# Sparsemax attention: two tiles' searches moved ahead, and the second group's candidate chain begun before the last two counts

## The chip, the core and the metric

The kernel runs on one core of one Trainium2 chip. It is one program for two decoder layers; the change touches one of its stages, the second layer's cross attention with sparsemax. The metric is the time of one execution on the device in microseconds. The core has five engines with a queue each: TensorE (PE, matrix products), VectorE (DVE), ScalarE (ACT), GpSimd (POOL) and SyncE (SP, which issues transfers). An engine works off its instructions in the order in which they are written, and waits where a semaphore has not been reached.

## The reference, cut to what matters

32 sequences, 100 queries each (S), 361 context rows each (S2), 16 heads of 16 (D = 256).

```python
def sparsemax(x):
    x = x - jnp.max(x, axis=-1, keepdims=True)
    zs = -jnp.sort(-x, axis=-1)
    ...
    support = zs > cssv / rho
    k = jnp.maximum(jnp.sum(support, axis=-1, keepdims=True), 1)
    tau = jnp.take_along_axis(cssv, k - 1, axis=-1) / k.astype(x.dtype)
    return jnp.clip(x - tau, 0.0)
...
qh = _split_heads(q @ Wq + bq)
kh = _split_heads(k @ Wk + bk)
vh = _split_heads(v @ Wv + bv)
scores = jnp.einsum('bhqd,bhkd->bhqk', qh, kh) * scale
attn = sparsemax(scores)
out = jnp.einsum('bhqk,bhkd->bhqd', attn, vh)
```

The result goes through Wo, is added to the stage's input and normalized by rows. Each row of 361 scores needs its own threshold tau, with the sum of max(x - tau, 0) equal to 1.

## The kernel before

The stage is `packed_sparse_attention`. The 16 x 100 rows of scores of one sequence lie in NT = 13 tiles of 128 rows (the last has 64) by 361. They form two groups: tiles 0 to 6 (group 0) and 7 to 12 (group 1). The threshold is found without a sort:

- `largest` (L3034) searches each tile in 8 parts of 45 or 46 scores with MAX8, 8 instructions per tile, and leaves 64 candidates per row. `half` splits a tile's search into two times 4.
- The chain of a group on VectorE: `bound` 0 and 1 (L3050, L3053) make a first threshold, `refine(.., 0, j)` and `refine(.., 1, j)` (L3063 to L3087) improve it twice. Ahead of each refine GpSimd subtracts the threshold from the candidates (`compare`, L2629). At the end stands nt0 (L3087).
- ScalarE's `cut` (L2888) subtracts nt0 from the whole tile, clips at 0 and sums. VectorE's `number` step 0 (L3096) counts what is left. `update` of step 0 or 2 (L3118, L3122, L3128) makes nu1 out of both.
- ScalarE's `excess` (L2896) and `sign` (L2904) sum and count above nu1; five tiles are counted by VectorE instead (`number` step 1: tiles 4, 5, 6, 11, 12). `update` of step 1 or 3 (L3117, L3118, L3122, L3126) makes nu2.
- GpSimd's `probability` (L2639) subtracts nu2 from each tile. TensorE turns the tiles (`turn`, L2763), ScalarE copies them out of PSUM (`copy_turned`, L2914), and TensorE multiplies by the values (`values`, L2775) and by Wo (`project_out`).

The scores come from `scores` on TensorE (L2749, L2745), in the order ORDER, through three PSUM banks: position pos needs the copy of position pos - 3. ScalarE's `copy_scores` (L2880) moves them to SBUF and counts in `z_in`, and `largest` waits for that count. The projections of a later sequence go through one bank: `turn_x`, `project_q`, `project_k` 0 and 1; `copy_x`, `copy_q`, `copy_k` 0 and 1 empty it. `project_k(.., 1)` waits for `copy_k(.., 0)`. `project_v` 0 to 2 share the bank `yo`, which `copy_v` on VectorE empties (L3023). `part_heads` on GpSimd (L2621, two instructions) spreads the queries by head.

Each engine has a `sequence(m, u)`, the body for one sequence of the batch (n = 2m + u), called by `passes`: a loop over m = 1 to 14 with u = 0 and 1, and the first and last bodies written out around it. In it `here` is work on (m, u), `behind` on the sequence before, `ahead` on the following one and `later` on the one after that. The first half of a body holds the chain of group 1 of (m, u), the second half the chain of group 0 of the following sequence. The order on each engine is written out by hand. What each wait names decides the rest: `update` step 1 and 3 wait for `total_done`, counted at the last excess of a group; `compare` for `tc_done`; `probability` of a group's first tile for nu2. GpSimd's order is: probabilities 7 to 12 of the sequence before, part_heads twice, compare of group 1 twice, add_bias, probabilities 0 to 6, compare of group 0 twice, norm. It is not changed.

## Time and profile before

| | us |
|---|---|
| three runs | 4212.95, 4183.81, 4180.03 |
| median | 4183.81 |
| the profiled execution | 4193.01 |
| its span | 4191.2 |
| VectorE busy, whole span | 2278.8 (54%) |
| ScalarE busy | 2184.1 (52%) |
| TensorE matmul busy | 3225.6 (77%) |

The stage runs from about 2180 to 3500 us, 32 bodies of some 40 us. In a row of a group "busy, mean ns | idle before <- who ended it" tells how long the engine stood just before these instructions. A row of a timeline gives the start, the duration, the engine, the line, what is written and read, and in brackets the idle time before. Names such as sa_s carry the stage's prefix; sa_nt is nt0, sa_nu is nu1 or nu2, sa_tc the threshold among the candidates, sa_sc the banks of the scores.

### The profile page before, as it was taken

To read this page: it belongs to the slowest core of one execution; us is meant where nothing else is said; L and a number is where in the kernel's file an instruction comes from. 1 tells how busy PE (TensorE), PEld (TensorE's weight loads), DVE (VectorE), ACT (ScalarE), POOL (GpSimd) and SP (SyncE) were. 2 spreads that over 40 slices of the span, in tenths; PEclk is the share of its full clock that TensorE was granted. 3 is DMA by queue.
4 is the path that set the end of the run, shared out by engine and by line. 5 is a ranking of instruction groups with operands and counts; after the bars stand their busy time and mean duration, and the time that the engine had idled before them with its cause. 6 is when DMAs were issued, how large, how long until landed. Compare 5 with 4: busy or idle time off the path is not lost. (4 is left out here: it accounts for less than half of the span.)

```text
span 4191.2 us, 84333 instructions
## 1 busy us (share of the span) xinstructions
PE 3225.6 (77%) x21166; PEld 1996.2 (48%) x21166; DVE 2278.8 (54%) x10359; ACT 2184.1 (52%) x6653; POOL 1448.4 (35%) x2228
## 2 busy tenths in 40 slices
PE   7999987888988824887767777877777775687772
PEld 5566665566666512444434444444444444344441
DVE  1222222566666684667648888888888882211112
ACT  3433333566566602666637877877777783221110
POOL 1111111355455545455523444444343441110005
PEclk9999998899999966768767887888888785899996
DMA  1000000111111011000010000000000003206773
GB/s 62 19 12 12 14 15 29 36 38 38 34 37 39 20 38 49 19 19 22 18 38 18 16 18 20 16 18 16 18 19 16 18 8 113 90 33 203 223 228 110
DMA packets 111870, 189.32 MB, mean 45 GB/s; under 512 B 11150, under 2 KB 95886, under 8 KB 105550
## 3 DMA queue, kind: packets, MB, share of 16 engines
q1 hardware_dynamic: 102094, 166.32, 12.9%
q10 hardware_dynamic: 7200, 14.68, 0.9%
q0 software_dynamic: 2400, 6.56, 0.5%
q14 instruction: 137, 1.12, 0.1%
q8 instruction: 39, 0.64, 0.1%
HBM read 149.90 MB, written 37.62 MB: 45 GB/s over the span
## 5 line engine op out<-in xcount | busy, mean ns | idle before, releaser
L3034 DVE MAX8 sa_cand<-sa_s 128x8 f32<-128x45 f32 (+3 forms) x3328 | 404.1, 191 | 34.7 <-ACT sa_s L2880 31.8
L852 ACT ACTIVATE ca_p<-ca_sm,ca_nb 100x361 f32<-100x361 f32 x512 | 301.9, 591 | 210.8 <-DVE ca_nb L936 209.8
L2763 PE MATMUL sa_tr<-sa_ident,sa_s 128*128 128x128 f32 (+3 forms) x1248 | 277.3, 339 | 167.9 <-POOL sa_s L2639 90.8
L672 POOL TENSOR_SCALAR ca_p<-ca_p,ca_rec 100x361 f32<-100x361 f32 x512 | 286.7, 579 | 345.2 <-DVE ca_rec L950 344.9
L2639 POOL TENSOR_SCALAR sa_s<-sa_s,sa_unit,sa_nu 128x361 f32<-128x361 f32 (+1 forms) x416 | 261.3, 644 | 306.3 <-DVE sa_nu L3126 306.3
L2763 PEld LDWEIGHTS sa_tr<-sa_ident,sa_s 128*128 128x128 f32 (+3 forms) x1248 | 185.5, 178 | 268.4 <-issue 257.5
L2888 ACT ACTIVATE sa_s<-sa_s,sa_nt 128x361 f32<-128x361 f32 (+1 forms) x416 | 244.3, 592 | 97.2 <-DVE sa_nt L3087 97.2
L936 DVE CUSTOM_DVE_ANT_0 ca_sm<-ca_sc,ca_mb 100x361 f32<-100x361 f32 x512 | 252.3, 526 | 69.4 <-PE ca_sc L759 56.4
L2896 ACT ACTIVATE sa_spare_a<-sa_s,sa_nu 128x361 bf16<-128x361 f32 (+1 forms) x416 | 247.2, 595 | 64.8 <-DVE sa_nu L3128 64.8
L2629 POOL TENSOR_TENSOR sa_over<-sa_cand,sa_tc 128x280 f32<-128x280 f32 (+3 forms) x128 | 99.3, 776 | 451.6 <-DVE sa_tc L3053 272.8
L2749 PE MATMUL sa_sc<-sa_kT,sa_qm 32*128 32x361 f32 (+3 forms) x768 | 227.2, 522 | 22.1 <-ACT sa_s L2880 21.5
L2914 ACT ACTIVATE sa_pT<-sa_tr 128x512 f32<-128x512 f32 (+5 forms) x384 | 182.7, 498 | 100.2 <-PE sa_tr L2763 97.2
L770 PEld LDWEIGHTS ca_tr<-ca_ident,ca_p 100*128 100x128 f32 (+1 forms) x1536 | 172.0, 154 | 102.3 <-issue 73.5
L770 PE MATMUL ca_tr<-ca_ident,ca_p 100*128 100x100 f32 (+1 forms) x1536 | 209.0, 260 | 3.2 <-POOL ca_p L672 2.5
L3096 DVE TENSOR_SCALAR_CACHE_REDUCE sa_spare_d<-sa_s 128x361 bf16<-128x361 f32 (+1 forms) x416 | 202.9, 517 | 0.1
L2728 PE MATMUL sa_yo<-sa_wv,sa_cTs 128*128 128x256 f32 (+1 forms) x384 | 157.9, 552 | 52.6 <-DVE sa_vm L3023 52.6
L465 DVE TENSOR_TENSOR ta_vpre<-ta_proj,ta_bvs 100x512 f32<-100x512 f32 x64 | 44.3, 692 | 276.0 <-PE ta_proj L337 275.9
L2880 ACT ACTIVATE sa_s<-sa_sc 128x361 f32<-128x361 f32 (+1 forms) x416 | 178.4, 464 | 20.1 <-PE sa_sc L2749 15.1
L1626 ACT ACTIVATE na_p<-na_sm,na_nb 100x100 f32<-100x100 f32 x512 | 186.8, 376 | 1.9 <-DVE na_nb L1691 0.7
L285 POOL TENSOR_SCALAR_AFFINE_SELECT ta_pT<-ta_pT 100x400 f32<-100x400 f32 x128 | 67.9, 542 | 318.4 <-ACT ta_pT L428 314.1
L1457 POOL TENSOR_TENSOR na_rs<-na_rs,na_half 100x32 f32<-100x32 f32 x32 | 174.5, 5453 | 2.7
L2749 PEld LDWEIGHTS sa_sc<-sa_kT,sa_qm 32*128 32x128 f32 (+3 forms) x768 | 82.9, 183 | 157.1 <-ACT sa_s L2880 94.2
(323 smaller groups left out, 7755.8 us busy)
## 6 DMA issues: line engine op xcount, KB each, us to landing
ea_we<-m_experts SPq DMA_DIRECT2D x40, 1024.0 KB, 6.6
ea_wd<-m_experts SPq DMA_DIRECT2D x40, 512.0 KB
ca_cTs<-cT SPq DMA_DIRECT2D x32, 361.0 KB
sa_cTs<-cT SPq DMA_DIRECT2D x32, 361.0 KB
rows_in<-me_zeros ACTq DMA_DIRECT2D x1, 7168.0 KB
ea_xe<-rows_in SPq DMA_DIRECT2D x40, 128.0 KB
rows_out<-ea_ye ACTq DMA_DIRECT2D x40, 128.0 KB
ca_ms<-mask SPq DMA_DIRECT2D x32, 141.0 KB
```

Source lines behind the costliest of these rows:

```text
L672: ins = pool.tensor_scalar(p[:, r, j, :], p[:, r, j, :], rec[:, r, j:j + 1], 1.0, ALU.mult, ALU.mult)
L770: mm = pe.transpose(tr[f % 2][0:kn, j * S:(j + 1) * S], p[:, r, j, k0:k0 + kn], ident[0:S, 0:S])
L852: act.activation(p[:, r, j, :], sm[:, r % 2, j, :], ACT.Exp, bias=nb[:, r % 2, j:j + 1], scale=-1.0, accum_out=den[:, r, j:j + 1]).then_in ...
L936: dve.tensor_tensor_reduce(sm[:, r % 2, j, :], sc[j][0:S, 0:S2], mb[:, u, :], -1 / 4, 3e38, ALU.add, ALU.min, nb[:, r % 2, j:j + 1]).then_ ...
L1626: act.activation(p[:, r, j, :], sm[:, r, j, :], ACT.Exp, bias=nb[:, r, j:j + 1], scale=-1.0, accum_out=den[:, r, j:j + 1]).then_inc(exp_do ...
L2639: pool.tensor_scalar(s[0:rows, u, i, :], s[0:rows, u, i, :], unit[0:rows, :], nu2[0:rows, i:i + 1], ALU.mult, ALU.add).then_inc(p_done.sem, 1)
L2749: mm = pe.matmul(bank[0:rows, 0:S2], qm[hr, u, P * i:P * i + rows], kT[hr, u, i // 7, :], start=True, stop=True)
L2763: mm = pe.transpose(tr[f % 2][0:kn, c0:c0 + rows], s[0:rows, u, i, k0:k0 + kn], ident[0:rows, 0:rows])
L2888: act.activation(s[0:rows, u, i, :], s[0:rows, u, i, :], ACT.Relu, bias=nt0[0:rows, i:i + 1], accum_out=total[0:rows, i:i + 1]).then_inc(r ...
L2896: ins = act.activation(spare_a[0:rows, i, :], s[0:rows, u, i, :], ACT.Relu, bias=nu1[0:rows, i:i + 1], accum_out=total[0:rows, i:i + 1])
L3034: ins = dve.max(cand[0:rows, i, q, :], s[0:rows, u, i, PART[q]:PART[q + 1]])
L3096: ins = dve.tensor_scalar(spare_d[0:rows, i, :], s[0:rows, u, i, :], u1[0:rows, i:i + 1] if step else 0.0, 0.0, ALU.is_gt, ALU.add, accum_ ...
```

## The change

On VectorE, the searches of positions 7 and 8 move from the head of a body to the end of the body before, between the steps of the chain of group 0. Group 1's searches now end sooner: its `bound` stands ahead of the counts of tiles 5 and 6, `copy_v(.., 0)` and `update` step 0; refine and update take turns. The searches of positions 0 and 1 of the following sequence move into group 1's chain. In the second half group 0's `bound` stands ahead of the count of tile 12 and of `update` step 2. On ScalarE, the copies of positions 0 to 2 stand among the excesses 1 to 3, and those of positions 7 to 9 among the excesses 9 to 11, ahead of both copy_k. On TensorE, scores 0 to 2 stand ahead of project_v(.., 1), scores 7 to 9 ahead of values(.., 0). The same instructions are issued per pass of the loop.

The diff, with its indentation cut by 12:

```diff
--- before.py
+++ after.py
@@ -2800,6 +2800,9 @@
             turn(*before, 2, t)
         for t in range(NK):
             turn(*before, 3, t)
+    if ahead:
+        for i in range(3):
+            scores(*following, i)
     if here:
         project_v(m, u, 1)
     if behind:
@@ -2807,10 +2810,6 @@
         values(*before, 3)
     if here:
         project_v(m, u, 2)
-    if ahead:
-        for i in range(3):
-            scores(*following, i)
-
     if ahead:
         for i in range(3, 7):
             scores(*following, i)
@@ -2826,6 +2825,10 @@
     if here:
         for t in range(NK):
             turn(m, u, 1, t)
+    if ahead:
+        for i in range(7, 10):
+            scores(*following, i)
+    if here:
         values(m, u, 0)
     if later:
         project_k(*second, 0)
@@ -2833,9 +2836,6 @@
         values(m, u, 1)
     if later:
         project_k(*second, 1)
-    if ahead:
-        for i in range(7, 10):
-            scores(*following, i)
 
 for u in range(2):
     turn_x(0, u)
@@ -2925,8 +2925,6 @@
     before = prev(m, u)
 
     if here:
-        for i in range(7, 10):
-            copy_scores(m, u, i)
         for i in range(3):
             cut(m, u, i)
             copy_scores(m, u, 10 + i)
@@ -2942,20 +2940,19 @@
     if behind:
         copy_turned(*before, 3, 1)
         copy_turned(*before, 3, 2)
-    if here:
-        for i in range(1, 4):
+    for i in range(1, 4):
+        if ahead:
+            copy_scores(*following, i - 1)
+        if here:
             excess(m, u, i)
             sign(m, u, i)
+    if here:
         excess(m, u, 4)
     if behind:
         copy_out(*before)
     if here:
         excess(m, u, 5)
         excess(m, u, 6)
-
-    if ahead:
-        for i in range(3):
-            copy_scores(*following, i)
     for i in range(4):
         if here:
             cut(m, u, 7 + i)
@@ -2979,25 +2976,26 @@
         copy_turned(m, u, 1, 1)
         sign(m, u, 8)
         copy_turned(m, u, 1, 2)
-        excess(m, u, 9)
-        sign(m, u, 9)
+    for i in range(7, 10):
+        if ahead:
+            copy_scores(*following, i)
+        if here:
+            excess(m, u, i + 2)
+            if i < 9:
+                sign(m, u, i + 2)
     if later:
         copy_k(*second, 0)
     if here:
-        excess(m, u, 10)
-        sign(m, u, 10)
-        excess(m, u, 11)
+        excess(m, u, 12)
     if later:
         copy_k(*second, 1)
-    if here:
-        excess(m, u, 12)
 
 for u in range(2):
     copy_x(0, u)
     copy_q(0, u)
     copy_k(0, u, 0)
     copy_k(0, u, 1)
-for i in range(7):
+for i in range(10):
     copy_scores(0, 0, i)
 passes(act, sequence)
 
@@ -3152,108 +3150,119 @@
     if behind:
         update(*before, 3, late, 0)
     if here:
-        largest(m, u, 7, 0)
+        largest(m, u, 9, 0)
     if behind:
         update(*before, 3, late, 1)
     if here:
-        largest(m, u, 7, 1)
+        largest(m, u, 9, 1)
     if behind:
         update(*before, 3, late, 2)
     if here:
-        largest(m, u, 8)
         number(m, u, 0, 0)
-        largest(m, u, 9)
+        largest(m, u, 10)
         number(m, u, 1, 0)
+        largest(m, u, 11)
         number(m, u, 2, 0)
-        largest(m, u, 10, 0)
+        largest(m, u, 12, 0)
         number(m, u, 3, 0)
         number(m, u, 4, 0)
-        largest(m, u, 10, 1)
+        largest(m, u, 12, 1)
+        bound(m, u, 1, second, 0)
         number(m, u, 5, 0)
+        bound(m, u, 1, second, 1)
         number(m, u, 6, 0)
+        copy_v(m, u, 0)
         update(m, u, 0, chain, 0)
-        largest(m, u, 11, 0)
+        refine(m, u, 1, 0, second, 0)
         update(m, u, 0, chain, 1)
-        largest(m, u, 11, 1)
+        refine(m, u, 1, 0, second, 1)
         update(m, u, 0, chain, 2)
-        largest(m, u, 12)
-        copy_v(m, u, 0)
-        bound(m, u, 1, second, 0)
+        refine(m, u, 1, 0, second, 2)
         number(m, u, 4, 1)
-        bound(m, u, 1, second, 1)
-        number(m, u, 5, 1)
-        refine(m, u, 1, 0, second, 0)
-        refine(m, u, 1, 0, second, 1)
-        refine(m, u, 1, 0, second, 2)
         copy_v(m, u, 1)
         refine(m, u, 1, 0, second, 3)
+        number(m, u, 5, 1)
         refine(m, u, 1, 0, second, 4)
         number(m, u, 6, 1)
+    if ahead:
+        largest(*following, 0)
+    if here:
         refine(m, u, 1, 1, second, 0)
         refine(m, u, 1, 1, second, 1)
+    if ahead:
+        largest(*following, 1, 0)
+    if here:
         refine(m, u, 1, 1, second, 2)
         copy_v(m, u, 2)
-        for j in range(3, 7):
-            refine(m, u, 1, 1, second, j)
-
+        refine(m, u, 1, 1, second, 3)
+        refine(m, u, 1, 1, second, 4)
+    if ahead:
+        largest(*following, 1, 1)
     if here:
+        refine(m, u, 1, 1, second, 5)
+        refine(m, u, 1, 1, second, 6)
         update(m, u, 1, chain, 0)
     if ahead:
-        largest(*following, 0, 0)
+        largest(*following, 2, 0)
     if here:
         update(m, u, 1, chain, 1)
     if ahead:
-        largest(*following, 0, 1)
+        largest(*following, 2, 1)
     if here:
         update(m, u, 1, chain, 2)
-    if ahead:
-        largest(*following, 1)
-    if here:
         number(m, u, 7, 0)
-    if ahead:
-        largest(*following, 2)
-    if here:
-        number(m, u, 8, 0)
-        number(m, u, 9, 0)
     if ahead:
         largest(*following, 3)
     if here:
-        number(m, u, 10, 0)
-        number(m, u, 11, 0)
+        number(m, u, 8, 0)
     if ahead:
-        largest(*following, 4, 0)
+        largest(*following, 4)
     if here:
-        number(m, u, 12, 0)
-        update(m, u, 2, chain, 0)
-    if ahead:
-        largest(*following, 4, 1)
-    if here:
-        update(m, u, 2, chain, 1)
+        number(m, u, 9, 0)
     if ahead:
         largest(*following, 5, 0)
     if here:
-        update(m, u, 2, chain, 2)
+        number(m, u, 10, 0)
+        number(m, u, 11, 0)
     if ahead:
         largest(*following, 5, 1)
         largest(*following, 6)
         bound(*following, 0, first, 0)
     if here:
+        number(m, u, 12, 0)
+    if ahead:
+        bound(*following, 0, first, 1)
+    if here:
+        update(m, u, 2, chain, 0)
+    if behind:
+        output(*before)
+    if here:
+        update(m, u, 2, chain, 1)
+    if ahead:
+        refine(*following, 0, 0, first, 0)
+    if here:
+        update(m, u, 2, chain, 2)
+    if ahead:
+        refine(*following, 0, 0, first, 1)
+    if here:
         number(m, u, 11, 1)
     if ahead:
-        bound(*following, 0, first, 1)
-    if behind:
-        output(*before)
-    if ahead:
-        refine(*following, 0, 0, first, 0)
-        refine(*following, 0, 0, first, 1)
         refine(*following, 0, 0, first, 2)
-        refine(*following, 0, 0, first, 3)
-        refine(*following, 0, 0, first, 4)
     if here:
         number(m, u, 12, 1)
     if ahead:
-        for j in range(7):
-            refine(*following, 0, 1, first, j)
+        refine(*following, 0, 0, first, 3)
+        refine(*following, 0, 0, first, 4)
+        largest(*following, 7)
+        refine(*following, 0, 1, first, 0)
+        refine(*following, 0, 1, first, 1)
+        largest(*following, 8, 0)
+        refine(*following, 0, 1, first, 2)
+        refine(*following, 0, 1, first, 3)
+        refine(*following, 0, 1, first, 4)
+        largest(*following, 8, 1)
+        refine(*following, 0, 1, first, 5)
+        refine(*following, 0, 1, first, 6)
 
 for i in range(7):
     largest(0, 0, i)
@@ -3264,6 +3273,8 @@
     refine(0, 0, 0, 0, first, j)
 for j in range(7):
     refine(0, 0, 0, 1, first, j)
+largest(0, 0, 7)
+largest(0, 0, 8)
 passes(dve, sequence)
 dve.wait_ge(*worst_done.at(B, 0))
 dve.tensor_reduce(top[:, :], worst[:, :], AX.X, ALU.max).then_inc(top_step, 1)
```

In the new program VectorE's functions stand 2 lines higher up (L3034 is L3032); those of ScalarE keep their numbers.

**VectorE, second half of a body**, from refine(.., 1, 0) of group 0 to the next body's first instructions. Before:

```order
L3096 TENSOR_SCALAR sa_spare_d,sa_count<-sa_s,sa_u 64x361
L3063 TENSOR_SCALAR sa_over<-sa_over 128x7x64
L3064 TENSOR_SCALAR sa_over<-sa_over 128x7x64
L3067 TENSOR_REDUCE sa_both<-sa_over 128x14
L3070 RECIPROCAL sa_few<-sa_both 128x7
L3073 SCALAR_TENSOR_TENSOR sa_shift<-sa_both,sa_few 128x7
L3076 TENSOR_TENSOR sa_tc<-sa_tc,sa_shift 128x7
L3083 TENSOR_SCALAR sa_low<-sa_tc 128x7
```

Now:

```order
L3074 TENSOR_TENSOR sa_tc<-sa_tc,sa_shift 128x7
L3032 MAX sa_cand<-sa_s 128x8 x8
L3061 TENSOR_SCALAR sa_over<-sa_over 128x7x64
L3062 TENSOR_SCALAR sa_over<-sa_over 128x7x64
L3065 TENSOR_REDUCE sa_both<-sa_over 128x14
L3032 MAX sa_cand<-sa_s 128x8 x4
L3068 RECIPROCAL sa_few<-sa_both 128x7
L3071 SCALAR_TENSOR_TENSOR sa_shift<-sa_both,sa_few 128x7
L3074 TENSOR_TENSOR sa_tc<-sa_tc,sa_shift 128x7
L3032 MAX sa_cand<-sa_s 128x8 x4
L3081 TENSOR_SCALAR sa_low<-sa_tc 128x7
```

The eight MAX8 ahead of L3061 are the search of position 7, the four and four behind it that of position 8.

**ScalarE, end of a body**, behind the excesses and signs of tiles 7 and 8 (L2896, L2904), up to the loop's branch. Before:

```order
L2914 ACTIVATE sa_pT<-sa_tr 105x384
L2896 ACTIVATE sa_spare_a,sa_total<-sa_s,sa_nu 128x361
L2904 ACTIVATE sa_spare_s,sa_signs<-sa_s,sa_nu 128x361
L2871 ACTIVATE sa_kT<-sa_proj,sa_bks 128x361
L2896 ACTIVATE sa_spare_a,sa_total<-sa_s,sa_nu 128x361
L2904 ACTIVATE sa_spare_s,sa_signs<-sa_s,sa_nu 128x361
L2896 ACTIVATE sa_spare_a,sa_total<-sa_s,sa_nu 128x361
L2871 ACTIVATE sa_kT<-sa_proj,sa_bks 128x361
L2896 ACTIVATE sa_spare_a,sa_total<-sa_s,sa_nu 64x361
L2597 UNCONDITIONAL_BRANCH
```

Now:

```order
L2914 ACTIVATE sa_pT<-sa_tr 105x384
L2880 ACTIVATE sa_s<-sa_sc 128x361
L2896 ACTIVATE sa_spare_a,sa_total<-sa_s,sa_nu 128x361
L2904 ACTIVATE sa_spare_s,sa_signs<-sa_s,sa_nu 128x361
L2880 ACTIVATE sa_s<-sa_sc 128x361
L2896 ACTIVATE sa_spare_a,sa_total<-sa_s,sa_nu 128x361
L2904 ACTIVATE sa_spare_s,sa_signs<-sa_s,sa_nu 128x361
L2880 ACTIVATE sa_s<-sa_sc 128x361
L2896 ACTIVATE sa_spare_a,sa_total<-sa_s,sa_nu 128x361
L2871 ACTIVATE sa_kT<-sa_proj,sa_bks 128x361
L2896 ACTIVATE sa_spare_a,sa_total<-sa_s,sa_nu 64x361
L2871 ACTIVATE sa_kT<-sa_proj,sa_bks 128x361
```

The three score copies (L2880) stand behind the last copy_turned, and one excess instead of an excess, a sign and an excess lies between the two copy_k (L2871).

**TensorE, first half of a body**, behind the transposes of the sequence before (L2763). Before:

```order
L2763 MATMUL sa_tr<-sa_ident,sa_s 105x64
L2728 MATMUL sa_yo<-sa_wv,sa_cTs 128x256 x2
L2775 MATMUL sa_ov<-sa_pT,sa_vm 32x100 x24
L2728 MATMUL sa_yo<-sa_wv,sa_cTs 105x256 x2
L2749 MATMUL sa_sc<-sa_kT,sa_qm 128x361 x6
```

Now:

```order
L2763 MATMUL sa_tr<-sa_ident,sa_s 105x64
L2749 MATMUL sa_sc<-sa_kT,sa_qm 128x361 x3
L2728 MATMUL sa_yo<-sa_wv,sa_cTs 128x256 x2
L2775 MATMUL sa_ov<-sa_pT,sa_vm 32x100 x24
L2728 MATMUL sa_yo<-sa_wv,sa_cTs 105x256 x2
L2749 MATMUL sa_sc<-sa_kT,sa_qm 128x361 x3
```

Three of the six scores (L2749) now stand ahead of project_v(.., 1), the first L2728.

## Rows read from the trace of the kernel before

**Rows 1.** Window table of two bodies: span, busy PE, PEld, DVE, ACT, POOL, clock, DMA
```profile
2800.10:2842.00 41.90, 31.55 (x209) 18.32 (x207) 33.81 (x197) 35.02 (x109) 16.86 (x25) 0.88 0.07 22
2842.00:2881.12 39.12, 30.24 (x195) 17.50 (x195) 33.92 (x196) 28.81 (x90) 16.86 (x25) 0.74 0.04 13
```

**Rows 2.** The same view of three short stretches
```profile
2809.00:2812.00 3.00, 2.11 (x6) 1.43 (x5) 2.69 (x18) 2.75 (x10) 0.55 (x1) 0.50 0.00 0
2816.00:2820.00 4.00, 2.56 (x12) 0.89 (x6) 3.12 (x12) 2.17 (x6) 0.17 (x1) 1.00 0.40 118
2842.00:2848.00 6.00, 2.80 (x9) 1.71 (x10) 5.80 (x43) 2.90 (x10) 4.12 (x7) 0.50 0.00 1
```

**Rows 3.** Groups of VectorE, 2250 to 3390 us: count, busy us, mean ns, idle before
```profile
L3063 DVE TENSOR_SCALAR sa_over<-sa_over 128x384 f32<-128x384 f32 x29 | 25.1, 867 | 15.6 <-POOL sa_over L2629 15.6
...
L3122 DVE SCALAR_TENSOR_TENSOR sa_u<-sa_total,sa_rec 128x7 f32<-128x7 f32 x28 | 16.3, 581 | 0.0
...
L3063 DVE TENSOR_SCALAR sa_over<-sa_over 128x448 f32<-128x448 f32 x28 | 11.9, 425 | 18.2 <-POOL sa_over L2629 18.2
...
L3070 DVE RECIPROCAL sa_few<-sa_both 128x7 f32<-128x7 f32 x56 | 11.3, 201 | 8.2
...
L3117 DVE TENSOR_SCALAR sa_count<-sa_signs 128x4 f32<-128x4 f32 x57 | 9.7, 170 | 43.4 <-issue 42.9
...
L3063 DVE TENSOR_SCALAR sa_over<-sa_over 128x240 f32<-128x240 f32 x28 | 8.0, 285 | 11.1 <-POOL sa_over L2629 11.1
```

**Rows 4.** VectorE's timeline in the first of these bodies: start us, us, instruction
```profile
2809.07 0.15 DVE L3128 TENSOR_SCALAR sa_nu<-sa_u 128x7 f32<-128x7 f32 x1
...
2813.66 0.42 DVE L3023 TENSOR_TENSOR sa_vm<-sa_yo,sa_bvs 128x256 f32<-128x256 f32 x1
...
2819.49 0.17 DVE L3117 TENSOR_SCALAR sa_count<-sa_signs 128x4 f32<-128x4 f32 x1
...
2827.89 0.15 DVE L3128 TENSOR_SCALAR sa_nu<-sa_u 128x6 f32<-128x6 f32 x1
```

**Rows 5.** GpSimd's timeline in the same body, with the idle time before in brackets
```profile
2801.95 3.77 POOL L2639 TENSOR_SCALAR sa_s<-sa_s,sa_unit,sa_nu 128x361 f32<-128x361 f32 x6 [2.82 <-DVE sa_nu L3126]
...
2805.69 3.00 POOL L2621 TENSOR_TENSOR sa_qm<-sa_qs,sa_hm 128x800 f32<-128x800 f32 x2
...
2811.45 0.63 POOL L2629 TENSOR_TENSOR sa_over<-sa_cand,sa_tc 128x240 f32<-128x240 f32 x1 [2.77 <-DVE sa_tc L3053]
```

**Rows 6.** Timeline of all engines at 2191 us, the stage's start
```profile
2191.30 1.52 POOL L2621 TENSOR_TENSOR sa_qm<-sa_qs,sa_hm 128x800 f32<-128x800 f32 x1
2191.38 1.73 DVE L3063 TENSOR_SCALAR sa_over<-sa_over 128x448 f32<-128x448 f32 x1 [1.15 <-POOL sa_over L2629]
```

**Rows 7.** ScalarE's timeline in the body of rows 4
```profile
2809.25 0.60 ACT L2896 ACTIVATE sa_spare_a<-sa_s,sa_nu 128x361 bf16<-128x361 f32 x1 [1.18 <-DVE sa_nu L3128]
...
2816.55 1.20 ACT L2880 ACTIVATE sa_s<-sa_sc 128x361 f32<-128x361 f32 x3
...
2828.07 0.59 ACT L2896 ACTIVATE sa_spare_a<-sa_s,sa_nu 128x361 bf16<-128x361 f32 x1 [1.18 <-DVE sa_nu L3128]
...
2831.97 0.60 ACT L2896 ACTIVATE sa_spare_a<-sa_s,sa_nu 128x361 bf16<-128x361 f32 x1
...
2836.33 1.18 ACT L2880 ACTIVATE sa_s<-sa_sc 128x361 f32<-128x361 f32 x3
```

**Rows 8.** TensorE's timeline in the body of rows 4
```profile
2807.97 1.58 PE L2763 MATMUL sa_tr<-sa_ident,sa_s 128*128 128x128 f32 x4 [0.27 <-ACT sa_pT L2914]
...
2810.44 2.08 PE L2728 MATMUL sa_yo<-sa_wv,sa_cTs 128*128 128x256 f32 x4 [0.89 <-DVE sa_vm L3023]
...
2815.65 0.88 PE L2749 MATMUL sa_sc<-sa_kT,sa_qm 32*128 32x361 f32 x6
...
2833.74 1.48 PE L2716 MATMUL sa_proj<-sa_cTs,sa_wk 128*128 128x361 f32 x4 [0.61 <-ACT sa_kT L2871]
```

## The prediction

> **What bounds the kernel now.** I read the window table first, to see what a pass of the loop costs: 81.02 us for two bodies (41.90 and 39.12 us) in which VectorE is busy 33.8 and 33.9 us; over the pair that is 67.7 us, against 63.8 of ScalarE, 61.8 of TensorE and 33.7 of GpSimd [rows 1]. Then the groups of VectorE over 1140 us of the stage [rows 3]: its listed idle time is 43.4 us at L3117, put down to "issue" (14 times, once per pass of the loop, 3.1 us each: no engine releases it), and 11.1 + 15.6 + 18.2 = 44.9 us at L3063, where it waits for GpSimd's compare (some 1.6 us per body). It never stands waiting for ScalarE or TensorE. The rest, some 3.6 us per body, are waits of 0.15 us between small operations of its own chain (8.2 us over 56 at L3070, [rows 3]). Then the timelines. VectorE's halves of a body run from L3117 to L3117: 2800.10, 2819.49, 2842.00, that is 19.4 us and 19.4 us + 3.1 us of the loop's turn [rows 1, 4]. ScalarE stands 1.2 us ahead of its first excess [rows 7] and GpSimd 2.8 us ahead of its probabilities [rows 5], both for VectorE. So VectorE's order is the bound, and what the edit can gain is its small gaps. The question is who is late next.
>
> I count t from the L3117 that opens a body, T from the one that opens its second half.
>
> **The VectorE work alone.** The edit adds and removes nothing within a pass: 104 MAX8, 13 + 5 counts, three copy_v. It only puts searches and counts between chain steps. By my count it covers six or seven of the small waits in a half (0.15 us each) and some 0.5 us of compare waits, 1.5 us in all: 17.9 us instead of 19.4 if nobody else were late. That would be 3.0 us per body. Four waits take its place.
>
> **First half, ScalarE's end.** nu1, which starts the seven excesses, is written at t = 9.1 now (L3128, 2809.07 + 0.15) [rows 4]. In the new order update(0, 1) and (0, 2) stand behind refine(.., 0), which waits for GpSimd's compare of the second group. GpSimd takes nu2 at t = 1.85, six probabilities (3.77 us) and two part_heads (3.00 us), so it is free at t = 8.6 and not before [rows 5]; the compare (0.63 us) can end at 9.25. Behind it come L3063, L3064, the update's two steps with the reduce between them (0.65 us): some 1.35 us, so nu1 at 10.6. There is one unknown. bound(.., 1) (L3053) would issue at t = 7.2, in the second part_heads (7.1 to 8.6). No row has L3053 beside one, but two show VectorE held up there: L3063 took 1.73 us at the stage's start beside a part_heads of 1.52 us [rows 6], against 0.43 in the loop, and L3122 takes 0.58 us in each body where it falls beside the second part_heads [rows 3]. So its price is 0 to 1.4 us for L3053, and as the compare was waiting anyway, 0 to 0.4 us for nu1. I take the block: nu1 at 11.0.
>
> The Trainium skill says of this in "SBUF — State Buffer", Who interferes with whom, that a tensor_scalar of VectorE can take both ports, and that whichever of it and a GpSimd operation comes second fully blocks. The rows above agree for the wide L3063; no row shows it for seven elements. By the rule the block is certain and this end of the first half 19.4 us; without it nu1 is at 10.6 and the end at 19.1.
>
> From nu1 ScalarE needs 7.3 us now to the end of the seventh excess (2809.25 to 2816.55) [rows 7]. The edit puts three score copies between them, 0.36 us apart (1.20 us for three), so 8.4 us: total_done at t = 19.4 (19.1 without the block). update(1) can't start before it. Now it starts at 19.39, with ScalarE ready at 16.6. **The saving of the first half is gone: 0 to 0.3 us.**
>
> **First half, TensorE's end.** scores 0 to 2 now stand ahead of project_v(1). The transposes end at 9.45 (2807.97 + 1.58) [rows 8]. The three scores took 0.88 us, at a granted clock of at most 1.00; at this place the stretch 2809 to 2812 shows 0.50 [rows 2, 8], so 0.9 to 1.8 us. project_v(1) took 2.08 us at that clock. So its copy_v(1) comes at t = 12.4 to 13.3 instead of 11.3 to 11.7 where VectorE gets to it; I take 12.8. What stands behind copy_v(1) on VectorE up to update(1) is 5.83 us now (2813.66 to 2819.49) [rows 4]; with count 5 (0.50), the searches of tiles 0 and 1 (16 MAX8, 1.75 us) added, and 1.5 us of waits covered, 6.6 us. That gives t = 19.4 too. Both ends agree: **first half 19.5 us**.
>
> **Second half.** VectorE reaches largest(7) at about T = 12.5: bound, output, refine 0 to 4 with both counts. It needs copy_scores(7). ScalarE does that behind excess 7, sign 7, copy_turned, copy_q, excess 8 and so on: 3.90 us behind its start (2828.07 to 2831.97) [rows 7]. That start waits for nu1 of the second group, now at T = 8.55 (2827.89 + 0.15 less 2819.49) [rows 4], but moved behind bound, output (1.2 us) and L3063: T = 10.3. So copy 7 ends at 10.3 + 3.9 + 0.46 = T 14.7, **and VectorE waits 2.2 us for it**. Of this 0.5 us come back, as the compare's wait is hidden behind it. 17.9 + 2.2 − 0.5 = **19.6 us against 19.4**. ScalarE's own end is close: from nu1 to the end of excess 12 it needs 8.3 us now (to 2836.33), + 1.08 for the copies − 0.45 for the copy_k that moved behind it + 0.2 for the accumulator: T = 19.4.
>
> **Across the bodies.** copy_k(.., 0) ends at T = 10.3 + 8.33 = 18.7. Only then may TensorE begin project_k(.., 1) (1.48 us, [rows 8]), which has just excess 12 to hide it now, where three operations of 1.7 us did. copy_k(.., 1) follows at 20.4 to 20.8, and cut 0 after it, 1.2 us behind VectorE's next start. The count of tile 0 waits 0.5 us, and everything that follows the cuts (copy_turned of the body before, the transposes) is late by 1.2 us: transposes end at 10.5, copy_v(1) at 13.8, **first half 20.4 us**. After the loop's turn, whose 3.1 us I leave as they are (same branch, same length of loop), this delay is hidden.
>
> **Sum** for a pass: 19.5 + 19.6 (u = 0), 20.4 + 19.6 + 3.1 (u = 1) = 82.2 to 82.3 against 81.0 (39.12, and 41.90 with the turn). 14 passes: +17 us, and 2 to 3 us for the four bodies outside the loop, in two of which the late copy_k counts too. The profiled execution's own time is 4193.0 us (span 4191.2), so 4213; the median of the three runs shown is 9 us lower, so I give 4184 + 20 = **4204 us**.
>
> **The rivals.**
> *A, the searches really cover the gaps.* copy 7 is there in time, and neither scores nor nu1 delay anyone: 3.0 us in each of 32 bodies, 4184 − 96 = 4088 us. Against it stands ScalarE's order, where copy 7 has 3.9 us of work ahead of it: it holds only if those excesses start 2 us earlier than nu1 lets them. 3%.
> *B, ScalarE alone limits* (first half 19.1 without the block, second 19.4, VectorE catching up in the loop's turn at 17.9 + 3.1): 78.6 us per pass, −2.5 us, over 16 passes −40 us, 4144 us. It needs TensorE's scores at the full clock and VectorE past copy 7 sooner. 7%.
> *C, both small delays absent* (no block, project_k(1) hidden): 19.3 + 19.6 + 19.3 + 22.7 = 80.9, −3 us in all, 4181 us. 22%.
> *D, slower.* One mechanism: TensorE stands idle for about 3 us ahead of project_k(.., 1), and its clock falls from 1.00 to 0.50, as it has in the stretch 2842 to 2848, where TensorE is busy for 2.80 of 6 us [rows 2]. Against it: in 2816 to 2820 it is busy for 2.56 of 4 us and stays at 1.00. Then project_k takes 2.9 us, copy_k and all cuts of u = 1 come 1.4 us later still: +2.7 us per pass, +43 us in all, 4227 us; with the scores and project_v at their late end (13.3) in both bodies, 0.5 us more each, 4243. It decides once project_k(1) takes over 2.4 us. 18%.
> *My forecast*, 50%: 4184 to 4215.
>
> **Numbers.** About 1% (42 us) is what a measurement of this kernel tells from no change. Faster by more than that: A and half of B, with some for what I have not seen: 0.09. Slower: most of D: 0.15. Range 4144 to 4238: B's end and D's are inside, A and the worst of D out. The forecast's own range is 4184 to 4215.
>
> **What would show it.** In the profile after: a wait at the searches of VectorE (MAX8) for ScalarE's score copy, of some 2 us per body, which is absent now; L3053 (L3051 then) lasting 1 to 1.5 us in the second group; ScalarE's wait ahead of its first excess grown from 1.2 to about 2.7 us; VectorE's waits at the compare mostly gone; a new wait of copy_v for TensorE. If VectorE's halves are 18 us, my ScalarE order is wrong and A holds; if the body of u = 1 takes over 44 us, D holds.

## The result and the profile after

| | before | after |
|---|---|---|
| median of the runs of one session, us | 4186.8 (4 runs, 4180.03 to 4212.95) | 4229.9 (4 runs, 4219.64 to 4239.82) |
| ratio to before | 1 | 1.0092, 95% interval 1.0057 to 1.0127 |
| the profiled execution, its span | 4193.01, 4191.2 | 4228.55, 4226.7 |
| from the first to the last start of a half in the stage | 1264.1 | 1313.7 |

The changed kernel is about 1% slower. All of it lies in the stage (+49.5 us). What lies ahead of the stage was 9.7 us shorter in this execution, though no instruction there changed; the first start of a half lies anywhere from 2200 to 2232 us in the profiled executions of all the kernels here, and 8 us apart in the two of one and the same kernel (e7, e10), so from here on passes of the loop are compared and not spans.

VectorE's halves of a body, from one `update(..)` count (L3117 before, L3115 after: the file is two lines shorter there) to the next, mean over the 14 passes:

| us | before | predicted | after |
|---|---|---|---|
| u = 0, first half | 19.66 | 19.5 | 19.36 |
| u = 0, second | 19.45 | 19.6 | 21.31 |
| u = 1, first | 19.40 | 20.4 | 20.06 |
| u = 1, second, with the loop's turn | 22.48 | 22.7 | 23.72 |
| a pass | 81.00 | 82.2 to 82.3 | 84.45 |

The window table of two bodies of after, u = 1 and then u = 0 (columns as in [rows 1]: span, busy PE, PEld, DVE, ACT, POOL, granted clock, DMA share, GB/s), with two stretches of 4 us in those bodies:

```profile
2814.09:2857.83 43.74, 34.00 (x212) 18.23 (x212) 32.67 (x195) 34.05 (x106) 17.11 (x25) 0.85 0.06 16
2857.83:2899.05 41.22, 34.30 (x196) 19.46 (x197) 33.67 (x195) 30.48 (x93) 16.70 (x25) 0.67 0.06 17
2892.00:2896.00 4.00, 4.00 (x30) 2.11 (x29) 2.81 (x12) 3.75 (x13) 1.57 (x4) 0.50 0.10 27
2845.00:2849.00 4.00, 2.55 (x23) 1.21 (x25) 1.98 (x8) 4.00 (x14) 1.43 (x3) 1.00 0.00 0
```

Against [rows 1] VectorE is busy for 66.3 us per pair instead of 67.7, and the pair takes 84.96 us instead of 81.02. So it does not do more; it waits more. Where, the groups of VectorE over 2250 to 3390 us tell (count, busy us, mean ns, idle before and who ended it), the same window as in [rows 3]:

```profile
L3032 DVE MAX8 sa_cand<-sa_s 128x8 f32<-128x45 f32 (+1 forms) x2810 | 345.6, 191 | 67.3 <-ACT sa_s L2880 65.9
L3094 DVE TENSOR_SCALAR_CACHE_REDUCE sa_spare_d<-sa_s 128x361 bf16<-128x361 f32 (+1 forms) x352 | 177.9, 517 | 12.2 <-ACT sa_s L2888 11.2
L3061 DVE TENSOR_SCALAR sa_over<-sa_over 128x280 f32<-128x280 f32 (+1 forms) x108 | 45.4, 420 | 0.9 <-POOL sa_over L2629 0.3
L3021 DVE TENSOR_TENSOR sa_vm<-sa_yo,sa_bvs 128x256 f32<-128x256 f32 (+1 forms) x81 | 33.0, 407 | 38.6 <-PE sa_yo L2728 38.5
L3115 DVE TENSOR_SCALAR sa_count<-sa_signs 128x4 f32<-128x4 f32 x54 | 9.2, 171 | 57.1 <-issue 42.5 <-ACT sa_spare_a L2896 14.1
```

The 44.9 us at the compare (L3063 in [rows 3], L3061 here) are gone. In their place stand 65.9 us of searches that wait for a score copy, 38.5 us of `copy_v` that waits for TensorE, 14.1 us of the update and 11.2 us of counts that wait for ScalarE: none of the four is there before, when VectorE never waited for ScalarE or TensorE.

### The profile page after: what moved, and what is told of

It reads as the page before. It is cut to its first block and busy times, and to the rows that moved or that the text cites. A ratio compares the mean times of both kernels' runs of the same rounds, so it can differ in the third digit from the quotient of the medians.

```text
span 4226.7 us, 84361 instructions
## 1 busy us (share of the span) xinstructions
PE 3259.2 (77%) x21166; PEld 2006.7 (47%) x21166; DVE 2257.9 (53%) x10359; ACT 2182.5 (52%) x6653; POOL 1454.1 (34%) x2228
## 5 line engine op out<-in xcount | busy, mean ns | idle before, releaser
L3032 DVE MAX8 sa_cand<-sa_s 128x8 f32<-128x45 f32 (+3 forms) x3328 | 408.1, 192 | 108.8 <-ACT sa_s L2880 107.3
L2763 PE MATMUL sa_tr<-sa_ident,sa_s 128*128 128x128 f32 (+3 forms) x1248 | 244.7, 315 | 170.7 <-ACT sa_pT L2914 137.5
L2896 ACT ACTIVATE sa_spare_a<-sa_s,sa_nu 128x361 bf16<-128x361 f32 (+1 forms) x416 | 248.0, 598 | 136.4 <-DVE sa_nu L3126 136.4
L2763 PEld LDWEIGHTS sa_tr<-sa_ident,sa_s 128*128 128x128 f32 (+3 forms) x1248 | 173.2, 168 | 244.3 <-issue 225.7
L2749 PE MATMUL sa_sc<-sa_kT,sa_qm 32*128 32x361 f32 (+3 forms) x768 | 268.1, 657 | 15.9 <-ACT sa_s L2880 15.9
L3094 DVE TENSOR_SCALAR_CACHE_REDUCE sa_spare_d<-sa_s 128x361 bf16<-128x361 f32 (+1 forms) x416 | 210.1, 517 | 14.3 <-ACT sa_s L2888 13.2
L2880 ACT ACTIVATE sa_s<-sa_sc 128x361 f32<-128x361 f32 (+1 forms) x416 | 192.4, 464 | 14.6 <-PE sa_sc L2745 7.7
L1535 PE MATMUL na_tr<-na_ident,na_p 100*100 100x100 f32 x512 | 85.4, 301 | 91.0 <-DVE na_p L1705 87.5
L1691 DVE CUSTOM_DVE_ANT_0 na_sm<-na_sc,na_cm 100x100 f32<-100x100 f32 x512 | 127.2, 261 | 49.3 <-PE na_sc L1524 30.8
```

The costliest lines, as they stand in the source:

```text
L2749: mm = pe.matmul(bank[0:rows, 0:S2], qm[hr, u, P * i:P * i + rows], kT[hr, u, i // 7, :], start=True, stop=True)
L2763: mm = pe.transpose(tr[f % 2][0:kn, c0:c0 + rows], s[0:rows, u, i, k0:k0 + kn], ident[0:rows, 0:rows])
L2880: act.activation(s[0:rows, u, i, :], sc[pos % SC][0:rows, 0:S2], ACT.Copy).then_inc(z_in.sem, 1)
L2896: ins = act.activation(spare_a[0:rows, i, :], s[0:rows, u, i, :], ACT.Relu, bias=nu1[0:rows, i:i + 1], accum_out=total[0:rows, i:i + 1])
L3032: ins = dve.max(cand[0:rows, i, q, :], s[0:rows, u, i, PART[q]:PART[q + 1]])
L3094: ins = dve.tensor_scalar(spare_d[0:rows, i, :], s[0:rows, u, i, :], u1[0:rows, i:i + 1] if step else 0.0, 0.0, ALU.is_gt, ALU.add, accum_ ...
```

## How a late nu1 comes back as a late search

The timeline of VectorE in the body of u = 0 (start, duration, and in brackets the idle time before); it answers to [rows 4]:

```profile
2857.83 0.17 DVE L3115 TENSOR_SCALAR sa_count<-sa_signs 128x4 f32<-128x4 f32 x1 [3.35 <-issue]
...
2868.50 0.16 DVE L3126 TENSOR_SCALAR sa_nu<-sa_u 128x7 f32<-128x7 f32 x1
...
2870.66 0.42 DVE L3021 TENSOR_TENSOR sa_vm<-sa_yo,sa_bvs 128x256 f32<-128x256 f32 x1 [1.26 <-PE sa_yo L2728]
...
2877.16 0.17 DVE L3115 TENSOR_SCALAR sa_count<-sa_signs 128x4 f32<-128x4 f32 x1
...
2887.98 0.16 DVE L3126 TENSOR_SCALAR sa_nu<-sa_u 128x6 f32<-128x6 f32 x1
...
2893.05 0.95 DVE L3032 MAX8 sa_cand<-sa_s 128x8 f32<-128x45 f32 x8 [2.64 <-ACT sa_s L2880]
...
2899.05 0.17 DVE L3115 TENSOR_SCALAR sa_count<-sa_signs 128x4 f32<-128x4 f32 x1 [0.99 <-ACT sa_spare_a L2896]
```

The same stretch on ScalarE ([rows 7] before):

```profile
2868.69 0.60 ACT L2896 ACTIVATE sa_spare_a<-sa_s,sa_nu 128x361 bf16<-128x361 f32 x1 [2.86 <-DVE sa_nu L3126]
...
2888.17 0.60 ACT L2896 ACTIVATE sa_spare_a<-sa_s,sa_nu 128x361 bf16<-128x361 f32 x1 [2.11 <-DVE sa_nu L3126]
...
2892.43 0.47 ACT L2880 ACTIVATE sa_s<-sa_sc 128x361 f32<-128x361 f32 x1 [0.25 <-PE sa_sc L2749]
...
2897.80 0.56 ACT L2871 ACTIVATE sa_kT<-sa_proj,sa_bks 128x361 f32<-128x361 f32 x1 [1.30 <-PE sa_proj L2716]
2898.26 0.59 ACT L2896 ACTIVATE sa_spare_a<-sa_s,sa_nu 64x361 bf16<-64x361 f32 x1
```

And on TensorE ([rows 8] before):

```profile
2889.95 0.94 PE L2763 MATMUL sa_tr<-sa_ident,sa_s 128*105 128x128 f32 x3 [3.01 <-ACT sa_pT L2914]
2890.82 3.08 PE L2749 MATMUL sa_sc<-sa_kT,sa_qm 64*128 64x361 f32 x6
2893.83 1.23 PE L2775 MATMUL sa_ov<-sa_pT,sa_vm 128*32 128x100 f32 x24
2894.99 2.78 PE L2716 MATMUL sa_proj<-sa_cTs,sa_wk 128*128 128x361 f32 x4
```

In the kernel before the same transposes came after 2.08 us of idle time:

```profile
2829.86 0.55 PE L2763 MATMUL sa_tr<-sa_ident,sa_s 128*105 128x128 f32 x3 [2.08 <-ACT sa_pT L2914]
```

Read together: nu1 of the second half is written at T = 10.8 instead of 8.4 (2887.98 less 2877.16). ScalarE has stood idle for 2.11 us by then, with `copy_turned(1, 0)` queued behind excess 7. TensorE waits 3.01 us for that copy. Its last transposes start at T = 12.8 in all 14 bodies of u = 0, and in the kernel before at T = 10.35 to 10.6 in eleven of them and at 12.0 in three: mostly 2.2 to 2.4 us later now, as nu1 is. In this body TensorE then comes back at the lower clock: the last transposes, the scores 7 to 9 and `project_k(.., 0)` take 0.94, 3.08 and 2.78 us where the body ahead of it (u = 1) shows 0.55, 1.68 and 1.48 at 1.00:

```profile
2846.67 0.55 PE L2763 MATMUL sa_tr<-sa_ident,sa_s 128*105 128x128 f32 x3 [1.45 <-ACT sa_pT L2914]
2847.14 1.68 PE L2749 MATMUL sa_sc<-sa_kT,sa_qm 64*128 64x361 f32 x6
2848.75 0.73 PE L2775 MATMUL sa_ov<-sa_pT,sa_vm 128*32 128x100 f32 x24
2849.41 1.48 PE L2716 MATMUL sa_proj<-sa_cTs,sa_wk 128*128 128x361 f32 x4
```

So copy 7 and both copy_k come late, search 7 waits 2.64 us, and excess 12, which stands behind `copy_k(.., 0)`, ends late too: the update waits for it.

The body of u = 1 shown here is not the rule for its kind. Over the 14 passes in the trace of after, the first project_k of a second half takes 2.3 to 2.8 us in all 14 bodies of u = 0 and in 12 of u = 1. Before, it did so in 5 of the 28, and then nobody waited for it. In one of the five the half took 19.45 us like every other of u = 0:

```profile
2466.70 0.94 PE L2763 MATMUL sa_tr<-sa_ident,sa_s 128*105 128x128 f32 x3 [2.15 <-ACT sa_pT L2914]
...
2468.72 2.78 PE L2716 MATMUL sa_proj<-sa_cTs,sa_wk 128*128 128x361 f32 x4
```

In after the scores 7 to 9, which search 7 is waiting for, stand in this stretch. The half of u = 0 goes with them: it takes 20.34 and 20.43 us in the two bodies where these scores took 1.94 and 2.02 us, and 21.4 to 21.9 us in the nine where they took 3.1 us.

The first half has a second cause, on GpSimd ([rows 5] before): `bound(.., 1)` now falls beside part_heads.

```profile
2865.11 1.36 DVE L3051 TENSOR_SCALAR sa_tc<-sa_level 128x6 f32<-128x6 f32 x1
```
```profile
2863.44 3.00 POOL L2621 TENSOR_TENSOR sa_qm<-sa_qs,sa_hm 128x800 f32<-128x800 f32 x2
2866.64 0.63 POOL L2629 TENSOR_TENSOR sa_over<-sa_cand,sa_tc 128x240 f32<-128x240 f32 x1 [0.21 <-DVE sa_tc L3051]
```

VectorE's L3051 ends at 2866.47, GpSimd's pair at 2866.44. Six elements took 1.36 us here and 0.92 us on average over 27 bodies; before, 0.157 us over 28. In e2 and e12, where searches 7 and 8 stand in the first half, this bound starts at t = 9.0, behind part_heads (over at t = 8.6), and takes 0.17 us.

## The experiments

The change has three parts: **S**, the searches of positions 0 and 1 in group 1's chain, with scores 0 to 2 and their copies ahead; **T**, searches 7 and 8 in group 0's chain, with scores and copies 7 to 9 and the place of copy_k; and **C**, the chain begun ahead of the last two counts (both `bound`) with update and refine step about. "nu1" is the mean time over the 14 passes from the start of a half to the start of the operation that writes nu1. **S'** is S in another form: scores 0 to 2 stand behind project_v(1) and ahead of `values(.., 2)` instead of ahead of project_v(1), and their copies one excess later.

| kernel | parts | median us (runs) | ratio to before, 95% | pass us | nu1, first and second half |
|---|---|---|---|---|---|
| before | none | 4186 to 4191 | 1 | 81.00 | 8.98, 8.39 |
| e7_before01 | S' | 4148.12 (4) | 0.9890, 0.9847 to 0.9934 | 78.35 | 8.98, 7.60 |
| e10_again | S' | 4140.60 (6) | 0.9885, 0.9855 to 0.9916 | 78.42 | 8.98, 7.60 |
| e11_search4 | S', T | 4135.54 (4) | 0.9876, 0.9849 to 0.9903 | 78.71 | 9.12, 7.61 |
| e12_chain | C | 4203.06 (10) | 1.0034, 1.0012 to 1.0056 | 82.36 | 11.23, 12.64 |
| e2_tail | S, C | 4186.27 (10) | 1.0005, 0.9983 to 1.0027 | 81.27 | 11.23, 10.70 |
| e3_head | T, C | 4244.60 (4) | 1.0136, 1.0084 to 1.0189 | 84.70 | 10.74, 12.64 |
| after | S, T, C | 4229.90 (4) | 1.0092, 1.0057 to 1.0127 | 84.45 | 10.75, 10.70 |

e1 to e4 undo or move one thing in the changed kernel; the others follow from what these leave open.

**e1_copyk**: is it the late copy_k? The order of copy_k and excesses as before, in the changed kernel.

```diff
-    for i in range(7, 10): copy_scores(i); excess(i + 2); sign
-    copy_k(0); excess(12); copy_k(1)
+    copy_scores(7); excess(9); sign(9); copy_k(0)
+    copy_scores(8); excess(10); sign(10); copy_scores(9); excess(11)
+    copy_k(1); excess(12)
```

> The changed kernel with ScalarE's two copy_k where they stood before: copy_k 0 ahead of excess 10, copy_k 1 ahead of excess 12; the score copies 7 to 9 stay among the excesses. Theory 1 (TensorE is late with project_k, because scores 7 to 9 now stand ahead of it and its clock is low in the body u = 0): copy_k 0 now waits ahead of excesses 10 to 12 instead of behind them, the second half of u = 0 grows from 21.3 to 22 to 23.5 us, the pass from 84.4 to 85 to 86, total +10 to +25 us. Rival (as in the prediction: only copy_k 1 behind excess 12 is late): cuts of u = 1 start in time, first half of u = 1 from 20.1 to 19.4, second half of u = 0 from 21.3 to 20.3, pass 82.7, total -28 us.

Measured: 4301.99 us (ratio 1.0274, 1.0225 to 1.0324), a pass of 88.91 us, second halves of 23.94 and 26.22. ScalarE's queue now waits for project_k at an earlier place, and copies 8 and 9, which VectorE wants, stand behind it:

```profile
L3039 DVE MAX8 sa_cand<-sa_s 128x8 f32<-128x45 f32 (+1 forms) x2672 | 328.7, 191 | 127.6 <-ACT sa_s L2880 126.1 <-issue 0.2
```

126.1 us against 65.9 of after, and a loss of 4.5 us per pass where theory 1 expected 0.6 to 1.6. In one place the rival was right: the first half of u = 1 falls from 20.06 to 19.41 us, so the late copy_k costs 0.65 us there. What a late copy_k costs in the second halves e1 doesn't show, because copies 8 and 9 now stand behind it; with the scores moved ahead on TensorE, copy_k is rightly put behind the copies.

**e2_tail**: part T undone.

```diff
-    scores(7..9); values(0); project_k(0); values(1); project_k(1)
+    values(0); project_k(0); values(1); project_k(1); scores(7..9)
     (copies 7 to 9, copy_k and searches 7 and 8 likewise as before)
```

> The changed kernel with its second-half part undone: searches 7 and 8 back at the head of a body, score copies 7 to 9 behind excess 12, scores 7 to 9 behind project_k 1, copy_k as before; the group-1 chain ahead of the counts, scores, copies and searches 0 to 2 and the chain of the second half stay. Theory 1 (the loss lies in the second half: VectorE waits for copy 7, TensorE late): second halves 21.3 and 20.6 + 3.1 go to about 19.0 and 17.4 + 3.1, first halves 19.7 to 20; pass 79, total 4150 to 4165 us, faster than the kernel before. Rival (the loss is in the first half: scores ahead of project_v, VectorE held up at bound): second halves hardly change the total, first halves rise by the 1.75 us of the two searches to 21.1 and 21.8; pass 82 to 83, total above 4200.

Measured: 4186.27 us, the time of before; a pass of 81.27. The sign was right and the hoped-for gain of the first part is absent: u = 0's second half takes 20.46 us instead of 19.45. This 1 us goes with the clock: in the three bodies where project_k(.., 0) took 1.48 us the half took 19.5 us, in the eleven where it took 2.2 to 2.8 us 20.3 to 21.8 us. VectorE's groups show what it waits for at the update:

```profile
L3117 DVE TENSOR_SCALAR sa_count<-sa_signs 128x4 f32<-128x4 f32 x56 | 9.5, 170 | 95.6 <-ACT sa_spare_a L2896 66.2 <-issue 29.3
```

66.2 us for the seventh and the last excess: ScalarE's chain from nu1 is now the bound of a half.

**e3_head**: part S undone.

```diff
-    refine(1,1,0..1) with largest(0), largest(1) between up to refine(1,1,6)
+    refine(1, 1, 3..6); update(1, ..) with largest(0), largest(1) between
     (scores 0 to 2 and their copies as before)
```

> The changed kernel with its first-half part undone: scores 0 to 2 back behind project_v 2, score copies 0 to 2 behind excess 6, searches 0 and 1 behind update 1; the rest as changed. Theory 1: copy_v 1 waits for TensorE no more and the first half falls to about 18.5 us, but the second half takes the two searches (1.75 us) and nu1 comes that much later, so copy 7 too: second half 21.5 to 23; pass 83 to 85, total within 20 us of the changed kernel. Rival (TensorE's scores ahead of project_v are the loss): pass back to 81 to 82, total 4190.

Measured: a pass of 84.70 us, 4244.60. The first halves fall to 18.21 and 18.41 us, and the second ones rise to 22.70 and 25.38: the 1.75 us of searches go back there. S is not what costs: beside T and C it still gains 0.25 us per pass.

**e4_early**: the updates of both groups ahead of the refine steps (and ahead of `output`), so that nu1 comes earlier; all else as in the changed kernel.

```diff
+    update(0, 0); copy_v(0); update(0, 1); update(0, 2)
     refine(1, 0, 0..1)
     ...
+    update(2, 0); update(2, 1); update(2, 2)
     output(before); refine(0, 0, 0..)
```

> The changed kernel with the updates whole and early: update(0, 0 to 2) ahead of refine(.., 0) in the first half, update(2, 0 to 2) ahead of output in the second. Theory 1 (nu1 starts ScalarE's excesses and with them everything that ends a half): nu1 1 us earlier in the first half, which TensorE's copy_v 1 then holds at 19.3; 1.2 to 1.7 us earlier in the second, of which ScalarE can use 0.6 to 1.0: pass 82.4 to 83, total -25 us against the changed kernel. Rival (VectorE's own amount of work bounds it): the uncovered small waits cost 0.5 us per body, total +15 us.

Measured: 4192.65 us (10 runs; ratio 1.0013, 0.9991 to 1.0036), a pass of 81.75, more than expected. nu1 comes at 10.12 and 9.44 instead of 10.75 and 10.70. The waits of after shrink at both ends, here VectorE's searches and ScalarE's first excess (116.6 us at L2896 in the changed kernel, 56.5 before):

```profile
L3032 DVE MAX8 sa_cand<-sa_s 128x8 f32<-128x45 f32 (+1 forms) x2912 | 357.8, 191 | 11.9 <-ACT sa_s L2880 7.9
```
```profile
L2896 ACT ACTIVATE sa_spare_a<-sa_s,sa_nu 128x361 bf16<-128x361 f32 (+1 forms) x362 | 217.4, 602 | 56.1 <-DVE sa_nu L3126 56.1
```

nu1 is 1.25 us earlier in the second half, and 1.75 us come back in u = 0's (21.31 to 19.56): the rest is TensorE, whose scores 7 to 9 take 1.68 us again in nine of the 14 bodies of u = 0 (a half of 19.3 us), and 2.9 to 3.0 us in the other five (20.1 us).

**e5_warm**: is the clock alone the cause? The transposes of turn(1, 1) issued seven times over (same result), which fills TensorE's idle time.

```diff
+    for _ in range(6 if (q, t) == (1, 1) else 0):
+        the transposes of this turn once more
```

> The changed kernel with added work on TensorE alone: the transposes of turn(.., 1, 1) are issued seven times instead of once (18 more), into the same bank, in the stretch where TensorE stands idle for about 3 us. ScalarE fetches that bank some 4 us later. Theory 2 (in the body u = 0 the granted clock falls to 0.50 in this idle stretch, and scores 7 to 9, the values and project_k 0 take twice as long, which delays copy_k 0, excess 12 and the cuts): clock 1.00 in the second half of u = 0, project_k 0 in 1.5 us instead of 2.8, second half of u = 0 from 21.3 to 20.2 us, pass 83.2, total -18 us. Rival (only the order on ScalarE counts, not the clock): same or slower by the added 2.5 us where TensorE is awaited, total 0 to +20 us.

Measured: a pass of 83.29 us (-1.16), u = 0's second half 20.71; the total, 4227.07 against 4229.90, can't be told from after. The clock over the window of the groups is back at before's 0.82 (0.79 in after):

```profile
2250.00:3390.00 1140.00, 930.26 (x6029) 550.43 (x6033) 912.96 (x5339) 874.64 (x2709) 469.32 (x684) 0.82 0.06 17
```

That is a third of the 3.45 us that a pass lost, and the clock's whole part is larger, because the added products hold the clock only in some bodies. Scores 7 to 9 of u = 0 take 1.68 us in eight of the 14, and their half takes 20.35 to 20.37 us; in the other six they take 2.6 to 3.0 us, and the half 21.0 to 21.4 us. So of the 1.86 us that this half lost (19.45 to 21.31) some 0.9 us are there at the full clock too, and the other 0.95 us are the clock's. nu1 hasn't moved (10.69 in the second half), and the last transposes start at T = 12.8 in all 14 as in after. The clock amplifies the delay and doesn't start it.

**e6_combo**: e4 with bound earlier, scores 0 to 2 behind project_v(1), and copies 0 to 2 one excess later (the form S').

```diff
-    scores(0..2); project_v(1)
+    project_v(1); scores(0..2)
-    number(3); number(4); largest(12, 1); bound(1, 0); number(5); bound(1, 1)
+    largest(12, 1); bound(1, 0); number(3); bound(1, 1); number(4); number(5)
```

> The changed kernel with what the theory asks for: the updates whole and early in both halves (as in e4), bound(.., 1) ahead of counts 3 and 4 so that it falls ahead of the second part_heads, TensorE's scores 0 to 2 behind project_v 1 instead of ahead of it, and score copies 0 to 2 one excess later. Theory (nu1 starts each half's end, TensorE's scores hold copy_v 1): nu1 at t = 9.0, copy_v 1 at t = 11.7, first halves 18.2 to 18.6 us instead of 19.4 and 20.1; second halves as in e4 (19.6 and 22.75) or better; pass 78.5 to 79.5, total 4145 to 4165 us, 0.5 to 1% faster than the kernel before. Rival (something else holds the halves, as the loop of ScalarE's own work): first halves stay at 19.3 and more, total 4190.

Measured: a miss, 4216.49 us and a pass of 82.80; first halves 20.30 and 20.18 instead of 18.4. nu1 of the first half comes at 10.83, later than in e4 (10.12). The second halves are those of e4 (19.58 and 22.74), and copy_v waits no more for TensorE (0.6 us over the window, 25.7 in e4, 38.5 in after). L3053 of six elements takes 1.74 us on average. Three edits are added to e4 here; e8 has one of them alone.

**e8_bound**: the changed kernel with that earlier bound alone.

> The changed kernel with one edit: search 12 whole and bound(.., 1) ahead of counts 3 and 4, so that L3051 issues at about t = 6.3, between no two operations of part_heads. Theory: L3051 of group 1 takes 0.16 us instead of 0.92, nu1 of the first half 0.3 us earlier, but copy_v 1 waits for TensorE as before, so the halves stay at 19.4 and 20.1: total within 8 us of the changed kernel. Rival (VectorE held up beside part_heads costs the first half): 0.4 us per body, -12 us or more.

Measured: 4241.27 us (1.0076 to 1.0154), a pass of 85.17, u = 0's first half 20.06 instead of 19.36, nu1 at 11.46. Both theories missed: L3051 took 1.76 us on average, not 0.16. The start is earlier and the end isn't:

```profile
2875.34 2.26 DVE L3051 TENSOR_SCALAR sa_tc<-sa_level 128x6 f32<-128x6 f32 x1
```
```profile
2874.57 3.00 POOL L2621 TENSOR_TENSOR sa_qm<-sa_qs,sa_hm 128x800 f32<-128x800 f32 x2
```

It is held for 2.26 us, to 2877.60, when both part_heads are over (2877.57), across the boundary between the two. Counted from the start of the half (2868.97) this is t = 8.6, as in after. VectorE stands for all that time with counts queued behind it. This is where e6's first halves went, at least in part.

**e7_before01**: the kernel before with part S' alone.

```diff
+    scores(0..2)         (TensorE, behind project_v(1), ahead of values(2))
+    copy_scores(0..2) among excess(2..4)             (ScalarE)
     refine(1, 1, 0..1) -> largest(0) ahead, largest(1) between and behind
     update(1, ..) -> largest(2); later ones one or two places earlier
```

> The kernel before with one part of the idea: only the searches 0 and 1 move into group 1's chain, with scores 0 to 2 behind project_v 1 and their copies among excesses 2 to 4; searches 7 to 9, their copies and scores, and all else as before. Theory: nothing waits for copy 7, nu1 of the second half comes 1.7 us earlier; first halves 19.8 (the 1.75 us of searches less the waits that they cover), second halves 18.5 to 19 and 20.2 with the loop's turn, pass 78.5 to 79.5, total 4150 to 4165. Rival (filling the chain's waits brings nothing, since ScalarE's and TensorE's work from nu1 on bounds the second half at 19.4): pass 81 to 82, total 4190 to 4200.

Measured: 4148.12 us, a pass of 78.35, 1.1% faster than before. The compare's wait:

```profile
L3064 DVE TENSOR_SCALAR sa_over<-sa_over 128x384 f32<-128x384 f32 (+1 forms) x117 | 48.8, 417 | 30.3 <-POOL sa_over L2629 30.3
```

30.3 us against the 44.9 of [rows 3], some 0.5 us per body, and no new wait. The gain shows in the second half: with two tiles' searches (1.75 us) gone from it, it gets to nu1 at 7.60 us instead of 8.39 (0.8 us earlier, not the 1.7 expected) and ends in u = 0 after 17.95 us instead of 19.45, and the first half, which took the searches in, grows by 0.33 us only. TensorE kept its clock: the first project_k of a second half takes 1.48 us in all 28.

**e9_scores**: e7 without VectorE's part, to see whether the earlier scores alone bring the gain. As in e7, the scores stand behind project_v(1), not ahead of it as the text below has it.

> The kernel before with the PE and ScalarE half of e7 alone: scores 0 to 2 ahead of project_v(1), their copies among excesses 2 to 4; VectorE's order stays that of before, so no search stands in group 1's chain. Theory (the gain of e7 is VectorE's: searches between steps of the second group's chain, which stands waiting for GpSimd's compare): without them the compare waits at L3063 stay as before (some 1.6 us per body), a pass stays at 80.5 to 81.5 us, the total at 4180 to 4200. Rival (the gain was ScalarE's and TensorE's, from scores and copies that come earlier and free the later ones): a pass of 78 to 79.5 us and a total near 4150, as e7 with 78.35 and 4148.

Measured: 4195.01 us (10 runs; ratio 1.0005, 0.9983 to 1.0027), a pass of 80.91, and the compare's wait as before:

```profile
L3064 DVE TENSOR_SCALAR sa_over<-sa_over 128x240 f32<-128x240 f32 (+1 forms) x114 | 54.5, 478 | 45.2 <-POOL sa_over L2629 45.2
```

The gain needs VectorE's order; the earlier scores and copies alone bring nothing. The rival fell.

**e10_again**: e7 once more, against chance.

> The kernel of e7 once more (the kernel before with only the searches of tiles 0 and 1 in the second group's chain, and the scores and copies that they need). Theory: its gain is a property of the order and not of one session: a ratio to before of 0.985 to 0.993, a pass of 78 to 78.8 us, second halves near 18 us in u = 0. Rival (the seven runs' difference was partly chance): a ratio of 0.995 to 1.0 and a pass over 80 us.

Measured: 4140.60 us, ratio 0.9885, a pass of 78.42, second halves of 17.94.

**e11_search4**: e7 with part T as well (S' and T); the updates and both bounds stay where they stood before.

> The kernel of e7 with the change's second-half part added: searches 7 and 8 between the steps of group 0's chain, scores 7 to 9 ahead of values 0, copies 7 to 9 among the excesses 9 to 11 and ahead of copy_k. The updates and both bounds stand where they stood before. Theory (the parts' costs add up; the second-half part costs 84.45 - 81.27 = 3.2 us per pass wherever it stands, because copy 7 comes too late and copy_k later): a pass of 81.3 to 81.8 us, total 4180 to 4195. Rival (it costs only where the late update holds nu1 of the second group back; with the update ahead of bound and output, copy 7 is there 2 us earlier, and search 7 covers gaps): a pass of 77.3 to 78.6 us, total 4120 to 4155, and no wait at MAX8.

Measured: 4135.54 us, a pass of 78.71, not 81.5. The parts don't add up: T costs 0.4 us per pass beside S' (e11 less e7), and 3.2 us beside S and C (after less e2). nu1 is at 7.61 in the second half, search 7 hardly waits and the compare's wait is a quarter of [rows 3]'s:

```profile
L3035 DVE MAX8 sa_cand<-sa_s 128x8 f32<-128x45 f32 (+1 forms) x3016 | 377.1, 192 | 12.6 <-ACT sa_s L2881 10.3
...
L3064 DVE TENSOR_SCALAR sa_over<-sa_over 128x448 f32<-128x448 f32 (+1 forms) x116 | 45.3, 391 | 11.4 <-POOL sa_over L2629 11.4
```

The rival's place was right and its size was not: it promised some more gain over e7, and e11 and e7 can't be told apart by the total. Both are 1.1 to 1.2% faster than before, and 2% faster than the changed kernel.

**e12_chain**: part C alone, both moves of searches undone.

> The change with both moves of searches undone: what is left is the chain's part alone, bound of either group ahead of the last counts, and refine and update step about, with the searches of positions 7 to 12 that much earlier in the body; TensorE and ScalarE as before. Theory (the parts add up; this one costs 81.27 - 78.35 = 2.9 us per pass through nu1, which is late): a pass of 83.5 to 84.2 us, ScalarE ahead of its first excess some 1.3 us per half later than before, total 4220 to 4235. Rival (it costs only together with the searches of tiles 0 and 1, which delay VectorE further): a pass of 80.5 to 81.5 us, total 4180 to 4195.

Measured: 4203.06 us (ratio 1.0012 to 1.0056), a pass of 82.36: between the two theories. VectorE comes to the update earlier and waits there for ScalarE, which waited for nu1:

```profile
L3115 DVE TENSOR_SCALAR sa_count<-sa_signs 128x4 f32<-128x4 f32 x55 | 9.4, 170 | 80.8 <-ACT sa_spare_a L2893 51.6 <-issue 29.2
```
```profile
2833.36 0.16 DVE L3126 TENSOR_SCALAR sa_nu<-sa_u 128x6 f32<-128x6 f32 x1
```
```profile
2835.34 0.59 PE L2763 MATMUL sa_tr<-sa_ident,sa_s 128*105 128x128 f32 x3 [3.35 <-ACT sa_pT L2911]
2837.01 2.51 PE L2716 MATMUL sa_proj<-sa_cTs,sa_wk 128*128 128x361 f32 x4
```

The half began at 2821.02, so nu1 is at T = 12.3 here, 3.9 us later than in [rows 4]. The chain of after's second half is there without any moved search: TensorE is idle for 3.35 us and its clock falls behind that, late enough that the transposes still take 0.59 us, but project_k 2.51. In the first halves nu1 is at 11.23, although bound is not held here, so nu1 can be this late without the block.

What the table says as a whole: C costs 1.4 us per pass alone. T costs 0.4 us beside S', 2.3 beside C (e3 less e12) and 3.2 beside S and C. Between the rows without C and those with it lie 2.9 us (e7 to e2) and 5.7 us (e11 to after), which is more than the change loses in all (3.45), but two things change there: C comes in, and S' becomes S, with scores 0 to 2 ahead of project_v(1). `copy_v` waits for TensorE for 14.9 us over the window in e2 and 38.5 in after, and for 0 and 0.6 us in e7 and e11, so a part of the 2.9 and 5.7 us may be the place of these scores; no run has it alone. e4 is clean: the updates whole and early, all else as in after, give back 2.7 of the 5.7 us.

## Why the prediction was right, and where it was not

The total came inside the range (4144 to 4238) and within the case "same", at its edge: +0.92%, interval 0.57 to 1.27%. The likeliest case's own range, 4184 to 4215, missed it by 15 us.

- **VectorE alone would need 17.9 us per half.** Right in kind: the compare's wait is gone in after (44.9 to 0.9 us), and where the others are hardly late, as in e11, second halves of 18.3 us are there in u = 0.
- **First half, block of bound.** Taken as 0 to 1.4 us for the operation; 0.92 us on average, up to 1.36 in the body shown. nu1 was put at 11.0 and came at 10.9, counted as there to the end of the operation. The Trainium skill ("SBUF — State Buffer", Who interferes with whom) says that a tensor_scalar of VectorE can take the ports that it shares with GpSimd, and that the one of the two that issues second is blocked until the other's instruction is over. The ends at 2866.47 and 2866.44 agree with it, for six elements too, and e8 adds that a pair of GpSimd's instructions back to back held VectorE over both (2.26 us).
- **First half, copy_v(1) at t = 12.8, end at 19.5.** It stands at 12.83 (2870.66), after a wait of 1.26 us; the end came at 19.36.
- **Second half, wait for copy 7.** Place and kind right: 2.2 us were expected and 2.28 to 2.64 measured. That the size fits is luck: both ends of the wait came late, VectorE at T = 13.2 instead of 12.5 in the body shown, and the end of copy 7 at T = 15.7 (2892.43 + 0.47) instead of 14.7. **The step that failed is the sum behind it, "17.9 + 2.2 − 0.5 = 19.6", with ScalarE's end at T = 19.4.** It took nu1 at 10.3 (10.85 on average, to the end of the operation) and left TensorE's operations at their durations of before. In the body of u = 0 shown, TensorE's scores 7 to 9 took 3.08 and project_k 2.78 us, copy_k(0) ended at T = 21.2 (2897.80 + 0.56) instead of 18.7, excess 12 at T = 21.7, and the mean half took 21.31 us: 1.7 us above the sum, of which 0.95 are the clock's by e5. In the body of u = 1 shown the clock held, and its half still took 23.72 us, 1.0 us more than the 22.7 predicted: search 7 starts 0.6 us later than predicted (2849.40 is T = 15.3), and the turn took 3.35 us instead of 3.1.
- **Across the bodies.** 20.4 us was expected for u = 1's first half and 20.06 came. The wait of count 0 and the late cuts are there, and as predicted almost only in the bodies of u = 1: 11.2 us at L3094 in 14 waits, 0.8 us each where 0.5 was expected.
- **Sum.** 82.25 was predicted for a pass, 84.45 came: 2.2 us × 14 = 31 us. The median is 26 us above the 4204 predicted. That the total lies in the range is owed to D, whose time the range was stretched to hold, and not to this sum.
- **The rivals.** D had the mechanism, a 3 us idle stretch of TensorE and the clock's fall, and the time (4227 to 4243), but not the place: it looked ahead of project_k(.., 1), where TensorE has no idle time in the body shown, and the stretch is ahead of the last transposes. Its own sign, a body of u = 1 over 44 us, did not come (20.06 + 23.72 = 43.78), because the loss fell on the second half of u = 0. The prediction tested the clock for one idle stretch and not for the one that its own late nu1 made. By the working for ScalarE (nu1 late by 1.9 us, copy_turned behind it) that stretch could have been seen: TensorE already stood there for 2.08 us (2829.86 of before). A was false for this change, since it needed excesses 2 us earlier. e11 gave it those (nu1 3.1 us earlier than in after) and got 2.3 us per pass, not the 6.0 of A. B and C fell; search 7 does wait.

What stays open: how the 3 us between e4 and e11 divide between `bound` ahead of the update, its being held beside part_heads, and scores 0 to 2 ahead of project_v(1). And why the clock falls at one pass of the same body and not at another; that u = 0's second half varies from 20.3 to 21.9 us in after follows from it.

## What to carry to other kernels

When work is put into the gaps of a dependent chain on one engine, look at which result of the chain another engine is waiting for, and keep it as early as it was: here the searches in the gaps gained 2.3 to 2.6 us per pass as long as the update stood ahead of the new chain. With the chain begun ahead of it and update and refine in turns the change lost 3.5 us, and the updates whole and early gave 2.7 of that back. Price a move in an interleaved schedule by the whole loop that it closes (nu1, excess, copy_turned, transposes, scores, copy, search), not by the first wait. And don't expect the prices of parts to add up: a part that costs 0.4 us in one company cost 3.2 in another. And look at the same body in several passes before it is called typical: the clock held in the one body of u = 1 shown here, and fell in 12 of the 14.

## What the runs showed of the hardware

- A tensor_scalar of VectorE with 128 × 6 elements, 0.157 us by itself, took 1.36 us beside one of GpSimd's tensor_tensor and 2.26 us beside two in a row (mean 0.92 in after, 1.74 in e6). It ended with the pair, at t = 8.6, whether it started at t = 7.3 (after) or 6.4 (e8): an earlier start made it longer and not sooner.
- TensorE's clock at this place is 1.00 (2.4 GHz) ahead of the idle stretch and 0.50 (1.2 GHz) behind it in many passes: after 3.01 us (2889.95 in after, scores 3.08 us instead of 1.68), and also after 2.15 us (2466.70 in before, project_k 2.78 us instead of 1.48). The length of this one stretch doesn't tell: in after 3.16 us left most of the scores at the full clock, and in e2 3.14 us left project_k at it.

```profile
2638.17 0.55 PE L2763 MATMUL sa_tr<-sa_ident,sa_s 128*105 128x128 f32 x3 [3.16 <-ACT sa_pT L2914]
2638.65 2.02 PE L2749 MATMUL sa_sc<-sa_kT,sa_qm 64*128 64x361 f32 x6
```
```profile
2866.61 0.55 PE L2763 MATMUL sa_tr<-sa_ident,sa_s 128*105 128x128 f32 x3 [3.14 <-ACT sa_pT L2914]
...
2867.74 1.48 PE L2716 MATMUL sa_proj<-sa_cTs,sa_wk 128*128 128x361 f32 x4
```

- The loop's turn costs VectorE 3.0 to 4.2 us of "issue" in every kernel (3.0 to 3.7 in before), where no other wait covers it, once per pass that branches back. The last pass, which doesn't, ends its second half of u = 1 after 19.58 us in before, against 22.5 to 23.2. No engine releases this wait and no run here took it apart.
